# Writing out the loops of a decoder layer's attentions, expert tiles and combining

## The chip, the cores and the metric

One core of a Trainium2 chip runs the whole kernel. Its engines are TensorE (PE; its weight loads are listed as PEld), VectorE (DVE), ScalarE (ACT), GpSimd (POOL) and SyncE (SP). Each has its own instruction stream, and they meet only at semaphores. The metric is the device time in microseconds. The kernel before takes 1984.65 us, the median of three runs between 1984.55 and 1985.22.

## The reference

One decoder layer with post-norm, on 32 sequences of 64 tokens of width 512 (2048 tokens), in float32:

```python
x = layernorm(x + self_attention(x))        # 32 heads of 16, causal, biases
x = layernorm(x + cross_attention(x, ctx))  # 32 query heads, 8 key heads of 128, rotary
x = layernorm(x + moe(x))

def moe(x):                                 # 16 experts, 4 per token, inner width 256
    scores = sigmoid(x @ gate_w.T) + bias
    topk_w, topk_idx = top_k(scores, 4)
    topk_w = topk_w / (sum(topk_w) + 1e-20)
    out = sum over the token's experts of topk_w * (silu(x @ Wg.T) * (x @ Wu.T)) @ Wd.T
    return out + (silu(x @ Sg.T) * (x @ Su.T)) @ Sd.T
```

## The kernel before, in words

Every float32 factor of a product is split into two float16 parts, and three matmuls stand for one product (`three_pass`, L382 to L384). The kernel runs in stages, one after the other:

1. `self_attention`: 4 groups of heads, and in each 4 steps of 512 tokens (`NG` = 4, `NQ` = 4).
2. `cross_attention`: 8 key heads with 4 query heads each (`NG` = 8), again 4 steps of 512 tokens.
3. `layernorm`, then `route_and_shared`: the gate, the lists of tokens per expert and the shared expert.
4. `experts`: 80 tiles of 128 gathered rows, in `NR` = 20 rounds of `U` = 4. Weights lie in a ring of four experts' places in SBUF. A tile's place in the ring is data: TensorE loads it into a register (`place_of`, L1996) and forms each weight slice's address from it.
5. `combine_and_normalise`: 16 tiles of 128 tokens, in 4 rounds of 4. For each tile a DMA brings four rows per token. VectorE and ScalarE weigh them, GpSimd adds ScalarE's two, and VectorE normalises the tile before.

The order of work on each engine is written by hand. In a step of the attentions TensorE's front work (projections, scores) is mixed with the back work (transposes, values, output product) of the step before. Loops over head groups, over rounds of tiles and over rounds of combining are hardware loops: `eng.Fori(a, b)` emits the body once per engine, followed by an addition on a counter and a compare-and-branch to the body's head. Each engine loops by itself and no barrier lies between iterations. The inner loop over `q` is Python's and is written out.

What a wait compares with is computed by class `Timeline`: each event has a place in the body, and `value(name, step)` gives `step.i * n + n + place + 1`. Where `step.i` is a loop's counter, this is an expression of a register, and it costs register instructions (ALU_OP, FUSED_REGOPS in the trace) ahead of the waiting instruction. Where `step.i` is a number, it is a constant. The same holds for addresses such as `m.place[0:1, bass.ds(column, 1)]`.

In self-attention the last group stands after the loop (`step(NG - 1, q, True)`), since it carries the first layer norm. In cross-attention the first group stands ahead of the loop for the same reason. So TensorE's loop passes are three in self-attention (two taken branches and an exit, L929), seven in cross-attention (six taken, L1389) and twenty in the experts (nineteen taken, L1998). GpSimd's steps in self-attention and SyncE's loading of experts are written out already.

Steps that the prediction follows: TensorE's tile in `experts`, where `gate_and_up` is followed by `turn_rows` (the next tile's tokens, L1459), by `down` of the tile before and by `turn_z` (L1992), which waits for VectorE's z (L1952). In combining they are ScalarE's `part` (Copy, L2089) and `root` (Sqrt, L2080), GpSimd's addition (L2073), and VectorE's L2129, L2139 and L2122.

Of the kernel before, what the change touches and what calls it, by code (L numbers as in the profile page):

```python
# [27 lines left out]
NQ = NT // TQ  # L28
# [80 lines left out]
def build(nc, x, xT, cT, maskf, wqT, wkT, wvT, b3, woT, bo, xwq, xwk, xwv, xwo,  # L109
# [3 lines left out]
    with top:  # L113
# [284 lines left out]
        def self_attention(prefetch_ctx, next_front, next_out, next_keys, next_values, ln):  # L398
# [3 lines left out]
            with ExitStack() as ctx:  # L402
# [67 lines left out]
                @block.sync  # L470
                def _(sp):
                    def front_weights(g):
                        for n, w in enumerate((wkT, wqT, wvT)):
                            sp.dma_start(raw_f[:, :, n * P:(n + 1) * P],
                                         w.rearrange("(k p) n -> p k n", p=P)[:, :, bass.ds(g * P, P)]).then_inc(s_rf, 16)
                    for h in range(2):
                        sp.dma_start(stage[0][:, 2 * h:2 * h + 2, :],
                                     xT.rearrange("(k p) t -> p k t", p=P)[:, 2 * h:2 * h + 2, 0:QT]).then_inc(s_st[h], 16)
                    front_weights(0)
                    sp.dma_start(ident[:, :], eye).then_inc(s_cn, 16)  # L480
                    sp.dma_start(caus[:, :], causal).then_inc(s_cn, 16)
                    sp.dma_start(par[:, :], parity).then_inc(s_cn, 16)
                    sp.dma_start(rawb[:, :, :], b3).then_inc(s_rb, 16)
                    sp.dma_start(raw_o, woT[0:P, :]).then_inc(s_ro, 16)
                    sp.wait_ge(s_pre_v, 1)
                    with sp.Fori(0, NG - 1) as i:
                        front_weights(i + 1)
                        sp.wait_ge(DV.sem, DV.value("wol", Step(i, 0)))
                        met(sp)
                        sp.dma_start(raw_o, woT[bass.ds((i + 1) * P, P), :]).then_inc(s_ro, 16)  # L490
                        sp.wait_ge(DV.sem, DV.value("wvl", Step(i, 3)))
                        met(sp)
                    next_front(sp, s_rf)
# [102 lines left out]
                def _(act):  # L596
# [74 lines left out]

                    with act.Fori(0, NG - 1) as i:
                        for q in range(NQ):
                            step(i, q)
                    for q in range(NQ):
                        step(NG - 1, q, True)
                    done = Step(None, 0)
# [10 lines left out]
                def _(dve):  # L688
# [103 lines left out]

                    with dve.Fori(0, NG - 1) as i:
                        for q in range(NQ):
                            step(i, q)
                    for q in range(NQ):
                        step(NG - 1, q, True)
                    done = Step(None, 0)
# [17 lines left out]
                def _(pe):  # L816
# [111 lines left out]

                    with pe.Fori(0, NG - 1) as i:  # L929
                        for q in range(NQ):  # L930
                            step(i, q)
                    for q in range(NQ):
                        step(NG - 1, q, True)
                    done = Step(None, 0)
# [16 lines left out]
        def cross_attention(cs, sn, s_cn, s_ro, PE, ln):  # L951
            NG = HKV
            FW = GQ * HD2 + 2 * HD2
            with ExitStack() as ctx:
# [54 lines left out]
                @block.sync  # L1009
                def _(sp):  # L1010
                    def front_weights(g):
                        c = 0
                        for w, n in ((xwq, GQ * HD2), (xwk, HD2), (xwv, HD2)):
                            sp.dma_start(raw_f[:, :, c:c + n],
                                         w.rearrange("(k p) n -> p k n", p=P)[:, :, bass.ds(g * n, n)]).then_inc(s_rf, 16)
                            c += n

                    def out_weights(g):
                        sp.dma_start(raw_o[:, :, :], xwo[bass.ds(g * GQ * HD2, GQ * HD2), :]
                                     .rearrange("(h p) n -> p h n", p=P)).then_inc(s_ro, 16)  # L1020
# [12 lines left out]
                    sp.sem_inc(s_cw, 32)  # L1033
                    sp.dma_start(rawc[:, :], ew[0:P, 0:CH]).then_inc(s_cr, 16)
                    with sp.Fori(0, NG) as i:
                        nxt = (i + 1) % NG
                        front_weights(nxt)
                        for q in range(NQ):
                            if q == 1:
                                sp.wait_ge(DV.sem, DV.value("wol", Step(i, 1)))  # L1040
                                met(sp)
                                out_weights(nxt)
                            sp.wait_ge(DV.sem, DV.value("cl", Step(i, q)))
                            met(sp)
# [13 lines left out]
                def _(pool):  # L1058
# [18 lines left out]

                    for q in range(NQ):
                        step(0, q, True)
                    with pool.Fori(1, NG) as i:  # L1080
                        for q in range(NQ):
                            step(i, q)

                @block.scalar
                def _(act):
# [75 lines left out]

                    for q in range(NQ):
                        step(0, q, True)
                    with act.Fori(1, NG) as i:
                        for q in range(NQ):
                            step(i, q)
                    back_p(Step(None, 0))
# [3 lines left out]
                def _(dve):  # L1171
# [114 lines left out]

                    for q in range(NQ):
                        step(0, q, True)
                    with dve.Fori(1, NG) as i:
                        for q in range(NQ):  # L1290
                            step(i, q)
                    st = Step(None, 0)
# [5 lines left out]
                def _(pe):  # L1298
# [87 lines left out]

                    for q in range(NQ):
                        step(0, q, True)
                    with pe.Fori(1, NG) as i:  # L1389
                        for q in range(NQ):  # L1390
                            step(i, q)
                    st = Step(None, 0)
# [442 lines left out]
        def experts(m):  # L1835
# [5 lines left out]
            with ExitStack() as ctx:  # L1841
# [40 lines left out]
                def _(pool):  # L1882
# [7 lines left out]
                    def store(st, i, first):  # L1890
# [10 lines left out]
                                                None).then_inc(s_yo[slot], 16)  # L1901
                    with pool.Fori(0, NR) as i:
                        for q in range(U):
# [14 lines left out]
                def _(act):  # L1918
                    AC.start(act)
                    with act.Fori(0, NR) as i:  # L1920
                        for q in range(U):
# [16 lines left out]
                def _(dve):  # L1938
# [9 lines left out]
                    with dve.Fori(0, NR) as i:  # L1948
                        for q in range(U):
# [14 lines left out]
                def _(pe):  # L1964
# [32 lines left out]

                    with pe.Fori(0, NR) as i:  # L1998
                        for q in range(U):
# [14 lines left out]
                            before = w  # L2014
                    down(Step(None, 0), weights(place_of(NTILES)))

        def combine_and_normalise(m):

            with ExitStack() as ctx:
# [17 lines left out]
                def _(sp):  # L2037
# [29 lines left out]
                def _(pool):  # L2067
                    PO.start(pool)
                    with pool.Fori(0, NQ) as i:  # L2069
                        for q in range(TQ):  # L2070
# [5 lines left out]
                def _(act):  # L2076
# [4 lines left out]
                    AC.start(act)  # L2081
                    with act.Fori(0, NQ) as i:
                        for q in range(TQ):
# [11 lines left out]
                def _(dve):  # L2095
# [18 lines left out]
                    def normalise(st, tile):  # L2114
# [8 lines left out]
                                                  ALU.subtract, ALU.mult), "norm", st)  # L2123
                    with dve.Fori(0, NQ) as i:
                        for q in range(TQ):
# [146 lines left out]
```

## Time and profile before

| | |
|---|---|
| median of three runs | 1984.65 us |
| the profiled execution | 1981.03 us, its span 1979.2 us |
| TensorE matmul busy | 1751.4 us (88%), 15496 instructions |
| VectorE busy | 1353.7 us (68%) |
| ScalarE busy | 940.9 us (48%) |
| GpSimd busy | 936.9 us (47%) |
| granted TensorE clock, mean | 0.95 |
| DMA | 200.13 MB, mean 101 GB/s |

The shares are means over stages that have different limits, so the rows below are taken stage by stage. Times are from the span's start. A granted clock of 1.00 is TensorE's upper level, 0.50 its lower. Matmuls are pipelined: the next starts before the end that is drawn for the one before it. Register, branch and semaphore instructions are not counted as busy; the view by line lists them, with a q behind the engine's name.

### The profile page before, as it was taken

The page shows a single profiled execution, that of the slowest core. Times are in us where ns is not written, and L with a number is a line of the kernel's source. Part 1 is how long each engine was busy: PE and PEld are TensorE (multiplying, and loading weights), DVE is VectorE, ACT ScalarE, POOL GpSimd, SP SyncE. Part 2 cuts the span into 40 slices and gives each one's busy share as a digit, 9 for nine tenths or more (in the row PEclk, how much of TensorE's full clock was granted, in tenths as well). Part 3 has the DMA queues.
Part 4 walks back from the last instruction along what each step waited for, and adds up shares of the span by engine and source line. Part 5 has one row for each costly group of instructions (what it writes and reads, how often), then busy time and mean ns, then how long its engine had stood idle before and what let it go on. Part 6 is the DMA issues. An engine that isn't in the chain of part 4 may idle for free. (4 is left out here: it accounts for less than half of the span.)

```text
span 1979.2 us, 45274 instructions
## 1 busy us (share of the span) xinstructions
PE 1751.4 (88%) x15496; PEld 1004.4 (51%) x15497; DVE 1353.7 (68%) x2069; ACT 940.9 (48%) x1565; POOL 936.9 (47%) x905
## 2 busy tenths in 40 slices
PE   6999999899999999999999999964678999999910
PEld 4666776555555555555555555533234554555500
DVE  5777888778788788887878888776753333333357
ACT  4556557654555654645545555434222333333334
POOL 6732024564554554645645546514344454445432
PEclk9999999999999999999999999986889999999965
DMA  9520011112221121221312203121313454643369
GB/s 265 124 44 24 3 56 50 54 65 76 75 90 61 65 97 54 97 78 41 118 44 85 86 33 118 65 72 54 106 64 129 141 205 168 220 151 111 111 235 311
DMA packets 82510, 200.13 MB, mean 101 GB/s; under 512 B 8704, under 2 KB 28544, under 8 KB 80320
## 3 DMA queue, kind: packets, MB, share of 16 engines
q1 hardware_dynamic: 63456, 136.89, 20.4%
q0 software_dynamic: 18912, 61.09, 9.9%
q8 instruction: 120, 1.97, 0.4%
q14 instruction: 22, 0.18, 0.0%
HBM read 141.86 MB, written 56.10 MB: 100 GB/s over the span
## 5 line engine op out<-in xcount | busy, mean ns | idle before, releaser
L382 PE MATMUL bank<-xhl,front_h 128*128 128x512 f16 x704 | 270.2, 384 | 20.5 <-DVEq L68 13.1
L383 PE MATMUL bank<-xhl,front_h 128*128 128x512 f16 x704 | 270.2, 384 | 0.0
L384 PE MATMUL bank<-xhl,front_l 128*128 128x512 f16 x704 | 269.9, 383 | 0.0
L1067 POOL TENSOR_TENSOR xa_xs<-xa_xs,sn 128x512 f32<-128x512 f32 x160 | 233.5, 1459 | 59.2 <-ACT xa_xs L1110 59.1
L1072 POOL TENSOR_TENSOR xa_rr<-xa_x,xa_xs 128x512 f32<-128x512 f32 x160 | 232.1, 1450 | 34.0 <-POOL xa_xs L1067 24.0
L1075 POOL TENSOR_TENSOR xa_sc<-xa_sc,xa_rs 128x1024 f32<-128x1024 f32 x32 | 62.2, 1945 | 374.2 <-DVE xa_rs L1281 374.2
L382 PE MATMUL bank<-out_h,xa_oh 128*128 128x512 f16 x512 | 194.2, 379 | 7.4 <-DVE xa_ol L1186 7.3
L383 PE MATMUL bank<-out_l,xa_oh 128*128 128x512 f16 x512 | 194.0, 379 | 0.0
L384 PE MATMUL bank<-out_h,xa_ol 128*128 128x512 f16 x512 | 194.0, 379 | 0.0
L1201 DVE TENSOR_TENSOR xa_x<-bank,cs 128x512 f32<-128x512 f32 x160 | 109.9, 688 | 84.7 <-ACT xa_xs L1110 82.5
L1109 ACT ACTIVATE xa_xs<-bank 64x512 f32<-64x512 f32 x160 | 95.0, 593 | 130.8 <-PE bank L384 127.2
L1952 DVE SCALAR_TENSOR_TENSOR mo_z<-bank,mo_sg 128x256 f32<-128x256 f32 x80 | 34.0, 425 | 179.7 <-ACT mo_sg L1924 174.3
L1900 POOL DMA_INDIRECT scratch_y<-mo_yo,mo_rows_to x81 | 80.0, 987 | 133.7 <-DVE mo_zl L1959 68.4
L1157 ACT ACTIVATE xa_sc<-xa_sc 128x512 f32<-128x512 f32 x64 | 40.2, 629 | 214.9 <-DVE xa_sc L1221 214.9
L382 PE MATMUL bank<-moe_ring,moe_xth 128*128 x320 | 123.1, 385 | 14.4 <-ACT mo_yo L1933 7.1
L1206 DVE TENSOR_TENSOR xa_rql<-xa_rr,xa_rqh 128x512 f16<-128x512 f32 x128 | 114.2, 892 | 14.4 <-ACT xa_rqh L1116 12.6
L383 PE MATMUL bank<-moe_ring,moe_xth 128*128 x320 | 122.3, 382 | 0.0
L384 PE MATMUL bank<-moe_ring,moe_xtl 128*128 x320 | 122.3, 382 | 0.0
L1924 ACT ACTIVATE mo_sg<-bank 128x256 f32<-128x256 f32 x80 | 30.7, 384 | 192.6 <-PE bank L384 190.1
L1193 DVE SCALAR_TENSOR_TENSOR acc<-bank,acc 128x512 f32<-128x512 f32 x128 | 86.1, 673 | 51.8 <-PE bank L384 51.8
L382 PEld LDWEIGHTS bank<-xhl,front_h 128*128 128x128 f16 x704 | 69.6, 99 | 100.6 <-DVEq L68 12.9
L384 PEld LDWEIGHTS bank<-xhl,front_l 128*128 128x128 f16 x704 | 69.6, 99 | 85.1 <-issue 3.8
(308 smaller groups left out, 4929.2 us busy)
## 6 DMA issues: line engine op xcount, KB each, us to landing
xa_rawc<-in_ew SPq DMA_DIRECT2D x33, 768.0 KB, 5.0
moe_ring<-scratch_w SPq DMA_DIRECT2D x16, 1536.0 KB
co_rows<-scratch_y SPq DMA_DIRECT2D x20, 1024.0 KB, 7.7
scratch_w<-xa_chunk_h SPq DMA_DIRECT2D x32, 384.0 KB, 2.3
scratch_w<-xa_chunk_l SPq DMA_DIRECT2D x32, 384.0 KB, 3.1
raw_front<-in_xwq SPq DMA_DIRECT2D x9, 1024.0 KB, 7.2
raw_out<-in_xwo SPq DMA_DIRECT2D x9, 1024.0 KB, 5.2
out<-raw_front SPq DMA_DIRECT2D x17, 256.0 KB, 6.7
```

The source lines that it names most:

```text
L382: pe.matmul(out_ap, ah, bh, start=start and m == 0, stop=False)
L383: pe.matmul(out_ap, ah, bl, start=False, stop=False)
L384: mm = pe.matmul(out_ap, al, bh, start=False, stop=stop and m == n - 1)
L1067: PO.mark(pool.tensor_tensor(xr, xr, sn[:, :].rearrange("p (a s) -> p a s", a=1) .to_broadcast([P, QT // S, S]), ALU.mult), f"sm{r}", st)
L1072: PO.mark(pool.tensor_tensor(rr[r % 2][:, :], x0[r % 3][:, :], xs[r % 3][:, :], ALU.add), f"ra{r}", st)
L1075: PO.mark(pool.tensor_tensor(s4, s4, rs[:, :, :].rearrange("p h (t a) -> p (h t) a", a=1) .to_broadcast([P, 16, S]), ALU.mult), "nm", st)
L1109: act.activation(xs[r % 3][0:64, :], src[64:128, :], ACT.Copy)
L1157: AC.mark(act.activation(s2, s2, ACT.Exp, scale=float(HD2) ** -0.5), f"ex{h}", st)
L1193: DV.mark(dve.scalar_tensor_tensor(row, home[f"w{t}"][:, :], 1 / (WS * OS), row, ALU.mult, ALU.add), f"w{t}", st)
L1201: DV.mark(dve.tensor_tensor(xr, home_of(r, st)[:, :].rearrange("p (a s) -> p a s", s=S), cs[:, :].rearrange("p (a s) -> p a s", a=1) .to_b ...
L1206: DV.mark(dve.tensor_tensor(rotated(rkl, rql, r), rr[r % 2][:, :].rearrange("p (a s) -> p a s", s=S), rotated(rkh, rqh, r), ALU.subtract), ...
L1900: pool.indirect_dma_start(ys[:, :], bass.IndirectOffsetOnAxis(rows_to[slot][:, 0:1], 0), yo[slot][:, :], None).then_inc(s_yo[slot], 16)
```

## The change

The hardware loops of the two attentions, of the experts' tiles and of combining become Python loops, on every engine that has one there. The loops of the two layer norm helpers stay. In both attentions the group that stood apart joins the others, with the same steps in the same order. In the experts TensorE no longer loads the tile's place a second time at the start of each round, nor once more after the last tile: it keeps the register.

```diff
@@ self_attention, SyncE
-                    with sp.Fori(0, NG - 1) as i:
+                    for i in range(NG - 1):
@@ self_attention, ScalarE, VectorE and TensorE alike
-                    with pe.Fori(0, NG - 1) as i:
+                    for i in range(NG):
                         for q in range(NQ):
-                            step(i, q)
-                    for q in range(NQ):
-                        step(NG - 1, q, True)
+                            step(i, q, i == NG - 1)
@@ cross_attention, SyncE
-                    with sp.Fori(0, NG) as i:
+                    for i in range(NG):
@@ cross_attention, GpSimd, ScalarE, VectorE and TensorE alike
-                    for q in range(NQ):
-                        step(0, q, True)
-                    with pe.Fori(1, NG) as i:
+                    for i in range(NG):
                         for q in range(NQ):
-                            step(i, q)
+                            step(i, q, i == 0)
@@ experts, GpSimd, ScalarE, VectorE and TensorE alike
-                    with pe.Fori(0, NR) as i:
+                    for i in range(NR):
@@ experts, TensorE
-                            if q == 0:
-                                before = weights(place_of(i * U))
+                            if (i, q) == (0, 0):
+                                before = weights(place_of(0))
...
-                    down(Step(None, 0), weights(place_of(NTILES)))
+                    down(Step(None, 0), before)
@@ combine_and_normalise, SyncE, GpSimd, ScalarE and VectorE alike
-                    with sp.Fori(0, NQ) as i:
+                    for i in range(NQ):
```

## Rows read from the trace of the kernel before

**Rows 1.** windows by stage: length, busy time per engine, PEclk, DMA share, GB/s
```profile
23.00:325.00 302.00, 284.83 (x4820) 200.01 (x4817) 238.98 (x414) 178.96 (x305) 116.04 (x159) 0.99 0.25 64
325.00:1313.00 988.00, 963.04 (x7632) 537.27 (x7630) 787.62 (x1010) 539.69 (x843) 522.79 (x352) 0.99 0.22 73
...
1500.00:1890.00 390.00, 376.65 (x2240) 199.35 (x2238) 140.38 (x280) 128.06 (x280) 192.31 (x323) 0.99 0.46 157
1900.00:1979.00 79.00, 0.00 (x0) 0.00 (x0) 59.95 (x116) 36.04 (x57) 22.94 (x16) 0.50 0.92 322
```

**Rows 2.** view by line, TensorE's loop branches: ns min/median/max, first and last start
```profile
L929 PEldq COMPARE_BRANCH  x3: 76/4243/4771, 91.0 to 243.7; - x3
...
L1389 PEldq COMPARE_BRANCH  x7: 83/3602/3903, 575.3 to 1300.6; - x7
...
L1998 PEldq COMPARE_BRANCH  x20: 76/208/228, 1517.6 to 1886.8; - x20
```

**Rows 3.** timeline of TensorE, where head groups begin: start us, us, engine line op
```profile
95.99 0.48 PE L382 MATMUL bank<-xhl,front_h 128*128 128x512 f16 x1 [2.92 <-DVE acc L728]
...
173.08 0.39 PE L382 MATMUL bank<-xhl,front_h 128*128 128x512 f16 x1 [2.38 <-DVE acc L728]
...
245.37 0.38 PE L384 MATMUL bank<-out_h,sa_ol 128*128 128x512 f16 x1
245.58 0.38 PE L382 MATMUL bank<-xhl,front_h 128*128 128x512 f16 x1
```

**Rows 4.** windows, behind the first edge (as rows 1)
```profile
96.00:100.00 4.00, 4.00 (x11) 1.47 (x12) 1.09 (x1) 0.00 (x0) 3.71 (x5) 0.57 0.30 89
```

**Rows 5.** waits of TensorE, 457 to 1300 us: us in total, times, longest
```profile
PE bank L382 <- DVE xa_sc L1221: 2.5, 5, 0.7
```

**Rows 6.** timeline of TensorE at two tile starts; last, the group's mean ns
```profile
1537.42 0.38 PE L1992 MATMUL bank<-ident,mo_z 128*128 128x128 f32 x2
1538.20 0.39 PE L382 MATMUL bank<-moe_ring,moe_xth 128*128 x1 [0.40 <-issue]
...
1542.54 0.38 PE L1992 MATMUL bank<-ident,mo_z 128*128 128x128 f32 x2
1542.85 0.39 PE L382 MATMUL bank<-moe_ring,moe_xth 128*128 x1
...
L1992 PE MATMUL bank<-ident,mo_z 128*128 128x128 f32 x160 | 30.8, 274 | 0.0
```

**Rows 7.** view by line, from z to the next tile (as rows 2)
```profile
L1952 DVE SCALAR_TENSOR_TENSOR mo_z<-bank,mo_sg x1: 424/424/424, 1541.4 to 1541.4; 128x256 f32<-128x256 f32 x1
...
L1996 PEldq TENSOR_LOAD <-moe_place x1: 301/301/301, 1542.0 to 1542.0; - x1
```

**Rows 8.** view by line, ScalarE in combining (columns as in rows 2)
```profile
L2089 ACT ACT_TABLE_LOAD  x4: 1283/1283/1283, 1905.7 to 1953.7; - x4
...
L2080 ACT ACT_TABLE_LOAD  x4: 1283/1283/1283, 1908.4 to 1956.4; - x4
```

**Rows 9.** timeline of VectorE in combining
```profile
1941.74 0.69 DVE L2139 TENSOR_TENSOR acc<-acc,raw_out 128x512 f32 x1 [1.06 <-POOL raw_out L2073]
...
1943.01 0.74 DVE L2129 SCALAR_TENSOR_TENSOR acc<-co_rows,moe_w,acc 128x512 f32 x1
...
1946.81 0.75 DVE L2129 SCALAR_TENSOR_TENSOR acc<-co_rows,moe_w,acc 128x512 f32 x1
```

**Rows 10.** DMA queues, 325 to 1313 us: packets, MB, share of 16 engines
```profile
q8 instruction: 70, 1.15, 0.5%
```

**Rows 11.** timeline of TensorE in the experts, at late weights
```profile
1682.55 0.62 PE L1459 MATMUL bank<-identh,moe_rows 128*128 128x128 f16 x8 [1.74 <-ACT moe_xth L1929]
```

**Rows 12.** timeline of TensorE, first 50 us; last, a window (as rows 1)
```profile
29.67 0.22 PE L383 MATMUL bank<-front_l,xhl 128*128 128x128 f16 x1 [2.21 <-issue]
...
48.22 0.20 PE L382 MATMUL bank<-sa_vbh,sa_pth 128*64 128x34 f16 x1 [1.61 <-issue]
...
47.00:52.00 5.00, 3.78 (x69) 3.74 (x70) 2.49 (x6) 0.59 (x1) 2.13 (x2) 0.66 1.02 355
```

More of the change, by code:

```diff
@@ L670, in step @@
                             AC.mark(act.activation(wo_h, raw_o, ACT.Copy, scale=WS), "woh", st)
-                    with act.Fori(0, NG - 1) as i:
+                    for i in range(NG):
                         for q in range(NQ):
-                            step(i, q)
-                    for q in range(NQ):
-                        step(NG - 1, q, True)
+                            step(i, q, i == NG - 1)
                     done = Step(None, 0)
@@ L791, in step @@
                             DV.mark(dve.scalar_tensor_tensor(wo_l, raw_o, WS, wo_h, ALU.mult, ALU.subtract), "wol", st)
-                    with dve.Fori(0, NG - 1) as i:
+                    for i in range(NG):
                         for q in range(NQ):
-                            step(i, q)
-                    for q in range(NQ):
-                        step(NG - 1, q, True)
+                            step(i, q, i == NG - 1)
                     done = Step(None, 0)
@@ L927, in step @@
                         back_out(st)
-                    with pe.Fori(0, NG - 1) as i:
+                    for i in range(NG):
                         for q in range(NQ):
-                            step(i, q)
-                    for q in range(NQ):
-                        step(NG - 1, q, True)
+                            step(i, q, i == NG - 1)
                     done = Step(None, 0)
@@ L1034, in _ @@
                     sp.dma_start(rawc[:, :], ew[0:P, 0:CH]).then_inc(s_cr, 16)
-                    with sp.Fori(0, NG) as i:
+                    for i in range(NG):
                         nxt = (i + 1) % NG
@@ L1076, in step @@
                                                    .to_broadcast([P, 16, S]), ALU.mult), "nm", st)
-                    for q in range(NQ):
-                        step(0, q, True)
-                    with pool.Fori(1, NG) as i:
+                    for i in range(NG):
                         for q in range(NQ):
-                            step(i, q)
+                            step(i, q, i == 0)
                 @block.scalar
@@ L1160, in step @@
                         AC.mark(act.activation(chunk_h[:, :], rawc[:, :], ACT.Copy, scale=WS), "ch", st)
-                    for q in range(NQ):
-                        step(0, q, True)
-                    with act.Fori(1, NG) as i:
+                    for i in range(NG):
                         for q in range(NQ):
-                            step(i, q)
+                            step(i, q, i == 0)
                     back_p(Step(None, 0))
@@ L1285, in step @@
                         DV.mark(dve.scalar_tensor_tensor(chunk_l[:, :], rawc[:, :], WS, chunk_h[:, :], ALU.mult, ALU.subtract), "cl", st)
-                    for q in range(NQ):
-                        step(0, q, True)
-                    with dve.Fori(1, NG) as i:
+                    for i in range(NG):
                         for q in range(NQ):
-                            step(i, q)
+                            step(i, q, i == 0)
                     st = Step(None, 0)
@@ L1385, in step @@
                             back_out(st, (2, 3))
-                    for q in range(NQ):
-                        step(0, q, True)
-                    with pe.Fori(1, NG) as i:
+                    for i in range(NG):
                         for q in range(NQ):
-                            step(i, q)
+                            step(i, q, i == 0)
                     st = Step(None, 0)
@@ L1901, in store @@
                                                 None).then_inc(s_yo[slot], 16)
-                    with pool.Fori(0, NR) as i:
+                    for i in range(NR):
                         for q in range(U):
@@ L1919, in _ @@
                     AC.start(act)
-                    with act.Fori(0, NR) as i:
+                    for i in range(NR):
                         for q in range(U):
@@ L1947, in out_rows @@
                         DV.mark(dve.tensor_copy(o[:, :], Y[(st.q + 1) % 2][:, :]), "y", st)
-                    with dve.Fori(0, NR) as i:
+                    for i in range(NR):
                         for q in range(U):
@@ L1996, in place_of @@
                         return pe.value_load(m.place[0:1, bass.ds(column, 1)], min_val=0, max_val=(RING - 1) * 2 * EW)
-                    with pe.Fori(0, NR) as i:
+                    for i in range(NR):
                         for q in range(U):
@@ L2068, in _ @@
                     PO.start(pool)
-                    with pool.Fori(0, NQ) as i:
+                    for i in range(NQ):
                         for q in range(TQ):
@@ L2081, in _ @@
                     AC.start(act)
-                    with act.Fori(0, NQ) as i:
+                    for i in range(NQ):
                         for q in range(TQ):
@@ L2123, in normalise @@
                                                   ALU.subtract, ALU.mult), "norm", st)
-                    with dve.Fori(0, NQ) as i:
+                    for i in range(NQ):
                         for q in range(TQ):
```

## The prediction

> **What bounds the kernel now.** Read the busy time by stage first, then TensorE's gaps inside each stage, since there it is over 94% busy in three of the four long stages [rows 1]: self-attention (23 to 325 us of the trace), cross-attention (325 to 1313) and the experts' tiles (1500 to 1890). Layer norm and routing (1313 to 1500) stay as they are. Combining (1900 to 1979) has no matmul; VectorE runs 60 of its 79 us. A loop's edge can move the end only where it holds up TensorE, or VectorE in combining. So the second view is the branch at each loop's end on TensorE's sequencer [rows 2], and the third the row in which the next step's first matmul starts [rows 3, 5, 6].
>
> The branch tells two things. Taken, it lasts 4.2 to 4.8 us in self-attention (the smallest of the three, 0.08, is the exit) and 3.6 us in the median in cross-attention, but 0.21 us in the experts' loop, whose body is short. Other engines' branches are not read as costs: what they delay would show on TensorE or, in combining, on VectorE.
>
> **Self-attention: two taken branches on TensorE.** After the first the next matmul comes 2.92 us late, after the second 2.38 [rows 3]. A 512-column matmul is drawn 0.38 us long but the next starts 0.22 later, as the two rows at 245.37 and 245.58 show, so each idle figure hides 0.16 more: 3.08 and 2.54, together 5.6. The rows name VectorE's addition (L728) as what ended the wait. I read that as the last semaphore in a list and not as the cause, for the third passage, at 245.58, has the same waits and the same splitting of weights behind it, its branch falls through, and it has no gap at all. The first gap is followed by 3.4 us in which the granted clock is one half (0.57 over the 4 us window) [rows 4], the lower of 1.2 and 2.4 GHz, after the array had stood still: half of 3.4 us, 1.7 more. Sum 7.3 us. Inside a step constants for the waits give nothing that I count, since the array has no gap there to close; a stall of a few tenths that VectorE ends would shrink by tenths at most.
>
> **Cross-attention: six taken branches.** TensorE's queue covers most of each 3.6 us: five gaps of together 2.5 us are left [rows 5], with the hidden 0.16 each 3.3; the sixth is below the view's threshold, at most 0.3. I take 3.6 us. VectorE, ScalarE and GpSimd shed register work behind TensorE, whose array is busy 963 of 988 us [rows 1]; that counts nothing, and if it ended TensorE's few other waits sooner it could give back some of these 25 us, which the low end holds.
>
> **Experts: nineteen taken branches and eighty tile starts.** At a loop's edge the first matmul of a tile starts 0.78 us after the pair of transposes before it (1537.42 to 1538.20), elsewhere 0.31 (1542.54 to 1542.85) [rows 6]: 0.47 us lost per edge, 19 edges, 8.9 us. The remaining 0.31 also has slack in it. The pair is drawn 0.38 long for two transposes of 0.27 each, so the second starts 0.11 after the first, and the next matmul could start at 0.22: 0.09 lost on each tile. The reason is on the sequencer. TensorE's sequencer sits at the wait for z until VectorE has written it (1541.4 plus 0.42, just over 1541.8), and only then computes the column of the ring's place, loads it (0.30 us) and goes on [rows 7]; the first matmul comes 1.0 us after z, while the array has 0.9 us of queued work. The computing of the column (some 0.10 with its distance to the next) goes when the column is a constant; the load itself, its bounds check and the address arithmetic for each weight slice stay. That just closes the gap: 80 times 0.09 is 7.2 us. Bounds of this term: 0, if the waits or the load become no earlier, and 7.2, as no more gap is there. I take 7.2, since the removed piece is as long as the gap. The reload of the place at each q = 0 goes too; it lies among queued matmuls and is worth nothing.
>
> Against this stands one stretch in which weights arrive late: at 1682.55 TensorE has waited 1.74 us behind ScalarE's copy, which itself waits for the ring's DMA by the code (L1926) [rows 11]. These loads run back to back at their own pace. Through their 30 us TensorE cannot keep what it gains there, six tiles of 0.09 and one edge of 0.47: minus 1.
>
> **Combining: three edges and the activation tables.** ScalarE loads a table twice per iteration, once before the first Copy (L2089) and once before the root (L2080), 1.28 us each, eight in all [rows 8]. Within an iteration Copy runs without a load after a root, so the root's table holds Copy. Only the loop's head, reached with two different tables, asks for the first load. Written out, one load before the first root is left of eight. On VectorE the edge shows as 1.06 us of idle before the addition at 1941.74, released by GpSimd [rows 9], which got its operands late from ScalarE. An iteration lasts 16.0 us (the four loads at L2089 stand from 1905.7 to 1953.7, 48.0 over three); a step without an edge 1946.81 minus 1943.01, 3.80 [rows 9]. Four of these are 15.2: 0.8 us for each of the three edges, 2.4. The first load (1905.74) lies ahead of the first Copy after the rows have landed, and goes too: 1.3 us on the first tile. Sum 3.7. What is late next is VectorE itself, whose seven operations fill the 3.80. The DMA is close behind: 1.31 MB per tile (1024 and 256 KB) in 3.80 us is 345 GB/s; the stage moves 322 GB/s at a share of 0.92 [rows 1], full 350, 3.75 us per tile. It allows the gain by a hair, and it is the next bound.
>
> **What straight code adds.** One queue carries instructions, 70 packets of together 1.15 MB in cross-attention [rows 10]; that stage ran 15,262 matmuls and loads [rows 1], 218 per packet. I read it as TensorE's code being fetched as it goes, in loops as well, while the experts' loop, short, stayed on the engine and will now be fetched. Twice in self-attention TensorE is idle in the middle of straight code for "issue", 2.21 us before 29.67 and 1.61 before 48.22, the second with a mean clock of 0.66 over 47 to 52 us [rows 12], which I read as late fetches. Written out, the packets' ends fall elsewhere in the steps of the second to fourth head groups. One more such stall with a half clock behind it is 1.8 and 1.7 us; two in the sixteen steps are seen, both early, so for the other twelve I allow half of one, minus 2 (bounds 0 and minus 7). The experts' 4,478 matmuls and loads [rows 1] are 21 packets, one in 18 us, far longer than the longest stall of a branch, 4.77: nothing there. The Trainium skill (Runtime: NRT & Kernel Launch, Instruction fetch mechanics) has a taken branch outside a two-block window force a fetch, which the branches of rows 2 agree with, but it also has sequential fetching mostly hidden; the rows at 29.67 and 48.22 disagree, if a fetch is their cause, and by the page the sum would be 2 us larger.
>
> Another of its rules speaks against the change: a compare-and-branch takes about 108 ns (Advanced Engine Details and Errata, Control Flow Timing). By that the experts' 19 edges would give 2.1 us and not 8.9, and the sum would be 20.9. The trace has 0.21 for the branch alone and 0.47 for the edge with what follows it in line, so the rows decide.
>
> **The sum.** 7.3 + 3.6 + 8.9 + 7.2 - 1 + 3.7 - 2 = 27.7 us. The profiled execution took 1981.03 us (span 1979.2); from it 1953.3. The median of the runs is 1984.65, 3.6 above it, with runs 0.7 apart. I carry the difference over: 1957.0 us.
>
> **Rivals.**
>
> A. VectorE's releases in the attentions are real: the branch hides behind them and without it the next matmul still waits for L728 or L1221, as rows 3 and 5 name them. Then 7.3 and 3.6 go, 16.8 is left, 1967.9 us. Against it stands the passage at 245.58.
>
> B. The tile start keeps its 0.09 (the load is paced by something else than the column's arithmetic): 20.5 left, 1964.2 us. For it: the two lengths compared differ by only 0.01.
>
> C. The loops' bodies hid fetching. With every engine streaming its code while the experts' DMA is 0.46 busy [rows 1], each of the 21 packets in the experts costs a stall as at 48.22 with the half clock behind it, 3.5 us: 74 lost against 27.7 won, 2031 us. It decides from 1.3 us per packet. Against it: cross-attention's 70 packets, with its DMA 0.22 busy, left the array idle for 25 us in all.
>
> D. The loops were cheap and the saved time returns in later waits of the same stages (late weights in the experts, DMA in combining): under 4 us left, about 1983.
>
> E. More than the sum: VectorE's chains in self-attention shorten as well, 35 us, about 1949.
>
> **How the numbers follow.** The forecast 0.55, A 0.12, B 0.16, C 0.05, D 0.04, E 0.08. 1957.0 is the likeliest. B and A reach to 1968; if both held, 9.6 us would be left, 1975, and I go most of the way there; E reaches to 1949. Range 1949 to 1972, which leaves out C, D and little else. A measurement of this kernel tells about 0.2%, 4 us, from no change. Faster 0.91, within it 0.04, slower 0.05.
>
> **What would show it.** No COMPARE_BRANCH of several microseconds on TensorE in the attentions; matmul following matmul at 0.22 us where the second and third head groups begin, and no half clock near 96 us. Tile period in the experts 4.56 us throughout, against 4.65 and 5.12. One table load in combining and an even 3.8 us step. The forecast is wrong if TensorE shows "issue" gaps of 1 to 4 us in the experts (C), if the gaps at the head groups stay with VectorE named (A), or if tile starts keep 0.31 us (B).

## The result and the profile after

The kernel after takes 1941.09 us in the median of six runs (1939.38 to 1943.79), the kernel before beside it 1984.54 (1980.39 to 1985.22): ratio 0.9786, interval [0.9773, 0.9798], 43.5 us less. The forecast was 1957.0 and its range 1949 to 1972, so the sign was right and the gain 16 us too small. The profiled execution of the kernel after took 1940.97 us, its span 1939.2, 40.0 less than the span before.

The table lays both profiled executions side by side. Each stretch runs between two matmuls that both kernels have. The last two columns give the same stretch in all traces of this study in which the stretch was left with its loops, and in which it was written out.

| stretch | before | after | gain | forecast | with loops | written out |
|---|---|---|---|---|---|---|
| start to self-attention's last step | 300.18 | 291.56 | 8.6 | 5.3 | 297.8 to 303.9 | 290.1 to 292.9 |
| cross-attention, second to last step | 879.63 | 871.96 | 7.7 | 3.6 | 879.1 to 879.8 | 872.0 |
| between the two | 94.29 | 94.29 | 0 | 0 | | |
| its last step, layer norm, to routing's logits | 97.75 | 98.38 | -0.6 | 0 | | |
| logits to the ranking's first matmul | 23.91 | 19.15 | 4.8 | 0 | see experiments | |
| from there to the experts' first matmul | 101.54 | 99.77 | 1.8 | 0 | 99.6 to 104.5, same code | |
| experts' matmuls | 392.85 | 378.54 | 14.3 | 15.1 | 390.8 to 393.2 | 376.8 to 378.7 |
| last matmul to the end | 89.07 | 85.52 | 3.6 | 3.7 | 88.8 to 90.5 | 84.6 to 85.6 |

The sum is 40.05 against 27.7. Windows by stage of the kernel after (columns as in [rows 1]) show self-attention in 293 us with 283.6 busy, and the clock whole in the experts:

```profile
23.00:316.00 293.00, 283.57 (x4828) 201.22 (x4827) 238.57 (x414) 178.99 (x306) 117.47 (x161) 0.99 0.27 67
316.00:1292.00 976.00, 956.92 (x7629) 535.50 (x7625) 811.72 (x1008) 537.63 (x841) 522.15 (x352) 1.00 0.22 73
...
1480.00:1854.00 374.00, 367.17 (x2235) 197.85 (x2233) 140.93 (x280) 128.18 (x280) 191.18 (x320) 1.00 0.48 164
1854.00:1939.00 85.00, 0.02 (x1) 0.00 (x0) 61.34 (x117) 26.01 (x50) 24.39 (x17) 0.53 0.87 305
```

The timeline of TensorE at the second head group, answering to [rows 3], has the next step's matmul 0.22 behind the last of the old one, and the window behind it, answering to [rows 4], has the whole clock:

```profile
93.34 0.38 PE L384 MATMUL bank<-out_h,sa_ol 128*128 128x512 f16 x1
93.56 0.38 PE L382 MATMUL bank<-xhl,front_h 128*128 128x512 f16 x1
...
93.50:97.50 4.00, 4.00 (x25) 2.32 (x23) 3.96 (x6) 2.33 (x5) 3.71 (x5) 1.00 0.01 4
```

A tile of the experts, answering to [rows 6], starts 0.22 after the pair of transposes and not 0.31. In the stretch of late weights, answering to [rows 11], TensorE now waits 1.27 and 1.75 us. The view says "issue" there, but each of the two matmuls starts 0.10 us behind the end of ScalarE's copy (`moe_xth`, ending at 1648.26 and 1655.65), and no packet of instructions is under way at these times. So this is still the wait for weights and not the stall that rival C names. First the tile's start, then the two waits:

```profile
1505.24 0.38 PE L1978 MATMUL bank<-ident,mo_z 128*128 128x128 f32 x2
1505.46 0.38 PE L382 MATMUL bank<-moe_ring,moe_xth 128*128 x1
...
1648.36 0.61 PE L1445 MATMUL bank<-identh,moe_rows 128*128 128x128 f16 x8 [1.27 <-issue]
...
1655.76 0.61 PE L1445 MATMUL bank<-identh,moe_rows 128*128 128x128 f16 x8 [1.75 <-issue]
```

In combining, ScalarE's groups of instructions (last the idle time before them) hold one table load, where [rows 8] had eight:

```profile
L2075 ACT ACTIVATE raw_out<-co_rows,moe_w 128x512 f32<-128x512 f32 x32 | 21.1, 707 | 17.5 <-DMA co_rows<-scratch_y 17.5
L2066 ACT ACTIVATE co_rs<-co_mv,eps 128x1 f32<-128x1 f32 x17 | 5.0, 295 | 36.2 <-DVE co_mv L2098 36.2
L2066 ACT ACT_TABLE_LOAD x1 | 1.3, 1283 | 0.0
```

What the forecast had not looked at is routing, which the change doesn't touch. In the kernel before, TensorE stood still in the middle of its 192 matmuls of 16 columns. The timeline, then the group of these matmuls in 1368 to 1384 us (count, busy us and mean ns, idle time before them by releaser), then windows (as [rows 1]):

```profile
1376.50 0.17 PE L384 MATMUL bank<-ro_gh,xhl 128*128 128x16 f16 x1
1380.28 0.19 PE L382 MATMUL bank<-ro_gh,xhl 128*128 128x16 f16 x1 [3.60 <-issue]
...
L382 PE MATMUL bank<-ro_gh,xhl 128*128 128x16 f16 x64 | 5.3, 174 | 6.5 <-issue 3.6 <-DVE ro_gl L1668 2.9
...
1374.00:1378.00 4.00, 2.68 (x101) 2.58 (x97) 0.00 (x0) 0.51 (x1) 3.35 (x1) 0.50 0.95 300
1378.00:1386.00 8.00, 5.72 (x28) 2.34 (x29) 4.57 (x30) 1.67 (x2) 0.00 (x0) 0.50 0.33 113
```

The same views of the kernel after have 0.35 us in place of 3.60, and the clock comes back sooner:

```profile
1360.12 0.17 PE L384 MATMUL bank<-ro_gh,xhl 128*128 128x16 f16 x1 [0.35 <-issue]
...
L384 PE MATMUL bank<-ro_gh,xhl 128*128 128x16 f16 x64 | 5.3, 174 | 0.4 <-issue 0.4
...
1358.00:1362.00 4.00, 3.65 (x132) 3.51 (x129) 0.00 (x0) 0.84 (x1) 3.69 (x1) 0.50 0.98 311
1362.00:1370.00 8.00, 8.00 (x33) 3.35 (x32) 7.37 (x56) 2.26 (x3) 0.00 (x0) 0.85 0.37 130
```

### The profile page after: what moved, and what is told of

Same layout as the page of the kernel before. It is cut to its first block and busy times, and to the rows that moved or that the text cites. A ratio compares the mean times of both kernels' runs of the same rounds, so it can differ in the third digit from the quotient of the medians.

```text
span 1939.2 us, 39745 instructions
## 1 busy us (share of the span) xinstructions
PE 1737.5 (90%) x15496; PEld 1003.0 (52%) x15496; DVE 1378.6 (71%) x2069; ACT 929.0 (48%) x1557; POOL 936.8 (48%) x905
## 5 line engine op out<-in xcount | busy, mean ns | idle before, releaser
L382 PE MATMUL bank<-xhl,front_h 128*128 128x512 f16 x704 | 269.3, 382 | 18.0 <-DVEq L68 14.3
L1196 DVE TENSOR_TENSOR xa_rql<-xa_rr,xa_rqh 128x512 f16<-128x512 f32 x128 | 144.5, 1129 | 12.7 <-ACT xa_rqh L1108 12.1
```

The lines of the kernel that those rows point to most:

```text
L382: pe.matmul(out_ap, ah, bh, start=start and m == 0, stop=False)
L1196: DV.mark(dve.tensor_tensor(rotated(rkl, rql, r), rr[r % 2][:, :].rearrange("p (a s) -> p a s", s=S), rotated(rkh, rqh, r), ALU.subtract), ...
```

## Experiments: one stage at a time

Each of the first four kernels is the kernel before with the loops of one stage written out, as the diff of the change does it there. Theory 1 is that the stages keep what the traces show; theory 2, that TensorE's code is fetched in packets, and where a packet ends decides the routing's stall.

> Only self-attention is written out (all four engines and SyncE there); the other loops stay. Theory 1 (each stage keeps what the two traces show for it): the last self-attention step starts 8.6 us earlier, time about 8.6 us below the kernel before, ratio 0.9957, if the code behind it keeps its stalls. Theory 2 (the place of TensorE's code in its 16 KB packets decides the stall of 3.75 us in the routing's 16-column matmuls): the written-out code moves everything behind it, so that stall may be gone here too though routing is untouched; then 12 us, ratio 0.994. The prediction on record: 5.3 us, 0.9973.

> Only cross-attention is written out. Theory 1: 7.9 us less (3.8 from the six branches, 3.4 from steps 1 of each kv head, 0.5 us each, in which TensorE waits shorter for VectorE's low half), ratio 0.9960. The prediction on record: 3.6 us, 0.9982. Theory 2 adds or not the 3.3 to 5 us of the routing's stall, by where the code comes to lie.

> Only the experts' tiles are written out. TensorE's code ahead of them doesn't move, so the routing's stall of 3.75 us stays under both theories. Theory 1: 14.3 us less, ratio 0.9928. The prediction on record: 15.1 us. If half the gain were due to the engines arriving in another phase from the routing stage (theory 3), under 8 us.

> Only combining is written out. Theory 1 and the prediction: 3.5 to 3.7 us less, ratio 0.9982. Rival: the saved table loads lie under the rows' transfers and only the edges count, 2.4 us, 0.9988. In no theory does anything ahead of combining move.

| written out | ratio, interval | median us | its own stretch, gain over before | logits' run, us |
|---|---|---|---|---|
| self-attention | 0.9927 [0.9907, 0.9947] | 1967.41 | 10.1 | 5.11 |
| cross-attention | 0.9937 [0.9917, 0.9958] | 1970.93 | 7.6 | 5.11 |
| experts | 0.9930 [0.9910, 0.9950] | 1968.92 | 14.1 | 8.58 |
| combining | 0.9979 [0.9964, 0.9994] | 1978.55 | 4.3 | 8.06 |

The kernel before ran 17 times beside them, 1973.1 to 1989.0 us, median 1981.62. The last column is the routing's 192 matmuls, 8.82 us in the kernel before and 5.61 in the kernel after. Where TensorE's code ahead of routing changed in length, the stall is gone; where it didn't, it stands. That is theory 2's mark, in a stage that the edit didn't touch. The gains of the stretches are differences of two single executions, and the traces with the loops differ among themselves by 6 us in self-attention's stretch, by 0.7 in cross-attention's and by 2.4 in the experts' (first table). The four gains add to 2.27% where the change has 2.14; the stall counts in two of them, and the intervals are wider than the rest.

## Experiments: the place of the code

Both kernels get semaphore increments on TensorE behind cross-attention's last matmul, and nothing else:

```
                     back_out(st)
+                    for _ in range(128):   # 159 in the kernel after
+                        met(pe)
```

> The kernel before, with 128 semaphore increments on TensorE's sequencer behind cross-attention's last matmul, where TensorE waits for layer norm anyway: half a 16 KB packet of 256 instructions. In the kernel before, the stall of 3.75 us stands at the 353rd instruction of the routing's 384 fast ones (192 matmuls of 16 columns and their weight loads, one instruction per 13.3 ns). Theory 2 (a packet ends there, and the next was asked for only 256 instructions, 3.4 us, earlier, and waits behind the weights' transfers): the packet's end moves to the 225th, the one behind it lies outside the fast run, no stall in the run, which takes 5.1 us and not 8.8, and from the last layer norm transposes to the ranking's first matmul 25.3 us pass and not 28.6 to 30.2. Rival (the stall belongs to the transfers or to a wait the trace doesn't show): it stays, near the same time after the run's start.

> The kernel after, with 159 such increments at the same place. There a gap of 0.50 us stands at the 256th instruction. Theory 2: the packets' ends move to the 97th and 353rd, as in the kernel before, and the stall of 3 to 3.8 us comes back, the run takes 8.1 to 8.8 us and not 5.6, the stretch 28.6 to 30.2 us and not 25.3, although every loop is written out. Rival (writing the loops out removed the stall in some other way): no stall, 25.3 us.

The groups of the same matmuls, first of the kernel before moved by 128 instructions, then of the kernel after moved by 159:

```profile
L382 PE MATMUL bank<-ro_gh,xhl 128*128 128x16 f16 x64 | 5.2, 174 | 3.2 <-DVE ro_gl L1670 3.2
```

```profile
L382 PE MATMUL bank<-ro_gh,xhl 128*128 128x16 f16 x64 | 5.3, 175 | 5.7 <-DVE ro_gl L1656 2.9 <-issue 2.8
```

The loops are all there in the first, and its run takes 5.11 us without a stall; the loops are all gone in the second, and the stall is back, the run 8.10 us. From the last transposes of layer norm to the ranking's first matmul pass 26.4 and 28.9 us (25.3 expected, and 28.6 to 30.2). So the stall belongs to the code's place and not to the loops. Over all 18 traces the rule holds: seven with TensorE's code at the old place have 8.1 to 8.9 us, ten with it elsewhere 5.1 to 6.6, and the one put back 8.10. In all eight that have the stall it stands before the 178th of the 192 matmuls (2.9 to 3.8 us from start to start). In the four whose TensorE code ahead of it is that of the kernel after, a shorter gap (0.5 to 1.5 us) stands before the 129th; the other six have none. The expectation was wrong on a side matter: the increments start 0.15 us apart, 19.5 and 24.4 us in all. The wait for layer norm hides only some 5 us of that, and the routing's matmuls began 14.7 and 19.9 us later. The times, 1994.21 and 1966.61 us, are so not the stall's price.

The next one moves the whole stream of the kernel after by 105 instructions from its head, to free self-attention's start, where the stalls of [rows 12] remain; beside it ran the kernel after, unchanged.

```
                     PE.start(pe)
+                    for _ in range(105):
+                        met(pe)
                     pe.wait_ge(s_q0l, 2)
```

> The kernel after with 105 semaphore increments ahead of TensorE's first wait, where it has over 15 us to wait for the first weights: all ends of packets lie 105 instructions earlier. In the kernel after the stalls at 31.42 us (2.46) and 49.03 (1.24) stand at the 449th and 962nd instruction of TensorE's stream, 513 apart, both one instruction off the same place in a packet of 256. Theory 2 (a packet's end inside a run of short matmuls costs the fetch's time less the run's): the ends move to places 344, 600, 856, 1112, of which only the first lies in a run, 4.2 us behind the one before it; both stalls and the routing's 0.50 go and none of over 1 us comes: 3 to 6 us less than the kernel after, about 1936. Rival (the stalls are the transfers', or others appear in their place): 1939 to 1943 or more.

> The kernel after, unchanged, beside the one with the shifted code on the same chip: 1938 to 1944 us by its six runs.

The timelines of TensorE in the kernel after (two rows) and in the moved one:

```profile
31.42 0.22 PE L384 MATMUL bank<-front_h,xhl 128*128 128x128 f16 x1 [2.24 <-issue]
...
49.03 0.20 PE L384 MATMUL bank<-sa_vbh,sa_ptl 128*64 128x34 f16 x1 [1.08 <-issue]
```

```profile
31.03 0.20 PE L383 MATMUL bank<-sa_vbl,sa_pth 128*64 128x34 f16 x1 [0.69 <-issue]
```

The two stalls are gone, one of 0.84 (0.69 of it drawn as idle above) and one of 0.60 us have come, and the routing's run is 5.12. The time didn't fall: 1945.38 us (1941.53 to 1946.34) against 1942.79 (1937.95 to 1944.36), ratios to the kernel before 0.9809 [0.9789, 0.9829] and 0.9788 [0.9766, 0.9810], which overlap. The trace says why: the increments take 0.15 us each there, more than the wait that should cover them, and the first matmul starts at 17.24 us and not at 13.10. The mechanism came out as told, the gain didn't, and a version that wins by it was not found.

## Experiments: which engine's loop

In cross-attention, written out on TensorE alone, on all but TensorE, and on GpSimd alone:

```
-                    with pe.Fori(1, NG) as i:      # pool.Fori for GpSimd alone
+                    for i in range(NG):
```

> Cross-attention written out on TensorE only; the other engines keep their loops. Measured by the trace, from the first matmul of the second step to that of the last (879.6 us in the kernel before, 872.0 written out on all). Theory 1 (two separate parts: TensorE's own branches 3.8 us, the other engines' shorter step 1 3.4 us): 875.8 us here. Rival (all of it is TensorE's, its own constants included): 872.0. Rival (the branch hides behind VectorE, as row A of the prediction had it): 879.

> Cross-attention written out on GpSimd, ScalarE, VectorE and SyncE, TensorE keeps its loop. Same stretch. Theory 1: 876.2 us, and each kv head's step 1 is 30.38 long instead of 30.86. Rival (all of it is TensorE's): 879.6 and 30.86.

> Cross-attention written out on GpSimd only. From the second step's first matmul to the last step's: 879.3 to 879.8 us in eight kernels with the loops, 878.3 with TensorE alone written out, 873.4 with all but TensorE. Theory 1a (GpSimd's rotation, which had 0.23 us of register work between two of its operations and hands VectorE its sums late, sets step 1 of each kv head): 875.5 to 876.5 here, step 1 at 30.43 and not 30.86. Theory 1b (VectorE's own loop does): 879 to 880 and 30.86.

Measured: 878.34, 873.43 and 873.40 us, against 879.6 and 872.0. TensorE's branches are worth 1.3 us while the other loops stay. Their cost moves rather than goes: the steps at an edge, 30.09 to 30.65 us long before, are 29.79, but the ones after them, mostly 29.79 before, are 30.28. GpSimd's loop alone is 6.2 of 7.7 us. Its timeline in the kernel before, where the addition follows the product 0.23 us after its end, and in the kernel after, where it follows in 0.08:

```profile
673.64 1.27 POOL L1067 TENSOR_TENSOR xa_xs<-xa_xs,sn 128x512 f32<-128x512 f32 x1 [1.52 <-ACT xa_xs L1110]
675.15 1.27 POOL L1072 TENSOR_TENSOR xa_rr<-xa_x,xa_xs 128x512 f32<-128x512 f32 x1 [0.23 <-POOL xa_xs L1067]
```

```profile
663.18 1.27 POOL L1061 TENSOR_TENSOR xa_xs<-xa_xs,sn 128x512 f32<-128x512 f32 x1 [1.53 <-ACT xa_xs L1102]
664.53 1.26 POOL L1066 TENSOR_TENSOR xa_rr<-xa_x,xa_xs 128x512 f32<-128x512 f32 x1
```

Between the two stand three register instructions that compute the counts for its waits. Five such pairs make a step, 0.75 us. TensorE feels it in step 1 of each key head (steps are counted from 0 here and below), where it waits for VectorE's low half at the output products. The waits of TensorE, 457 to 1250 us, first before, then with only GpSimd written out:

```profile
PE bank L382 <- DVE xa_ol L1186: 5.9, 8, 1.3
```

```profile
PE bank L382 <- DVE xa_ol L1184: 4.4, 8, 1.1
```

Step 1 goes from 30.86 to 30.43 us, as theory 1a said, and the steps at an edge are 29.9 to 30.0, nearly without it, which the theory had not expected: the row of [rows 5] (VectorE L1221, 2.5 us) and one at L1178 (1.2 us) are gone from this view, though TensorE still takes its six branches. The trace of before has VectorE's name on these waits; the slow link is one engine further up.

Self-attention written out on TensorE only, and combining on ScalarE only:

> Self-attention written out on TensorE only. From the start of the second step to that of the last: 263.5 to 266.4 us in seven kernels with the loops, 254.4 to 255.2 in three written out on all. Theory 1, the prediction's (the two taken branches on TensorE with the half clock behind them, 7.3 us): 257 to 259, with steps 3 and 7 at 17.9 to 18.2. Rival (the branches of VectorE, ScalarE and GpSimd hold TensorE when its own is gone, as in cross-attention): steps 3 to 8 keep half or more of the 8 to 11 us, 260 to 263. Row A of the prediction (it all stays with VectorE): 263 or more.

> Combining written out on ScalarE only. From the last matmul to the end: 89.1 to 90.5 us in eight kernels with the loops, 84.8 and 85.5 written out on all. Theory 1 (the table loads and ScalarE's own branch make the edge late): 84.8 to 86 us. Rival (only the first table load counts, 1.3 us, the edges are VectorE's, GpSimd's and SyncE's branches): 87.6 to 88.5.

Self-attention: 259.93 us, at the lower end of the rival's range, but its step 1 was odd (23.94 us; in the other traces 18.5 to 22.5). Steps 3 to 8, which hold both edges, tell more: 116.6 us in the mean of ten traces with the loops (112.6 to 118.7), 109.5 with TensorE alone written out, steps 3 and 7 at 18.28 and 17.99, and 107.8 in the mean of seven written out on all (107.6 to 108.1). TensorE's two branches with their half clock are 7.1 us (7.3 were put on them), the other engines' loops 1.7. The 109.5 is one trace, and the ten with the loops spread over 6 us, so the parts are good to a few us; steps 3 and 7 alone, 19.7 to 21.4 us in those ten, bear out that both edges go. Rival A's reading falls here. Combining: 86.50 us, between theory and rival: of some 4.3 us ScalarE gives 3, the other loops the rest. ScalarE's groups already have the one table load that the kernel after has:

```profile
L2089 ACT ACTIVATE raw_out<-co_rows,moe_w 128x512 f32<-128x512 f32 x32 | 21.1, 707 | 17.1 <-DMA co_rows<-scratch_y 17.1
L2080 ACT ACTIVATE co_rs<-co_mv,eps 128x1 f32<-128x1 f32 x17 | 5.0, 295 | 37.5 <-DVE co_mv L2112 37.5
L2080 ACT ACT_TABLE_LOAD x1 | 1.3, 1283 | 0.0
```

## Experiments: the experts' edge and tile start

> The experts' tiles written out on TensorE only. Measured by the trace, from the first matmul on the ring's weights to the last matmul: 391.1 to 393.2 us in five kernels with the loop, 376.8 to 378.7 in three with all engines written out. Theory 1 (edge and tile start are TensorE's own, as the prediction had it): 377 to 379 us. Rival (as cross-attention showed, a good part of an edge is the other engines' branches): the 19 edges keep about half of their 0.47 us, 381 to 384 us.

> The kernel after, but with the column of the ring's place computed from a register on TensorE for every tile again (register times 4 plus a constant, the register is zero), then loaded as before. Same stretch, 376.8 to 378.6 us in the kernel after. Theory 1 (the arithmetic of the column after z is what cost 0.09 us per tile, 80 tiles): 384 to 386 us, and tile periods of 4.64. Rival (the load's other parts or the registers in the waits): 377 to 379.

> The kernel after, but TensorE's loop over the experts' tiles has two iterations, each with half of the tiles written out, so that the column of the ring's place and the counts in its waits come from a register again, with one edge in place of nineteen. First matmul on the ring's weights to the last matmul, 376.8 to 378.7 us written out. Theory 1 (the register instruction of 0.11 us between z and the place's load costs each tile its 0.09 us): 384 to 387 us, most tile periods 4.64. Rival (the 0.09 comes from the distance to the branch or from something else): 377 to 380, periods 4.55.

The second and third change TensorE's loop in the kernel after:

```
-                    for i in range(NR):
+                    with pe.Fori(0, 1) as zero:             # second kernel
+                      for i in range(NR):
...
-                            w = weights(place_of(i * U + q + 1))
+                            w = weights(place_of(zero * U + (i * U + q + 1)))
```

```
-                    for i in range(NR):
+                    with pe.Fori(0, 2) as half:             # third kernel
+                      for ii in range(NR // 2):
+                        i = half * (NR // 2) + ii
```

TensorE alone: 378.53 us, all of the 14.3; here no other engine's loop counts. The second: 376.79, which looked like the rival but told nothing, for its trace has no register instruction ahead of the place's load; the constant zero had been folded away. The third has that instruction again: most periods are 4.64 to 4.68 us in place of 4.55, and every fourth tile, which reloads the old place, 4.77. So a register instruction of 0.11 us between z and the load costs each tile 0.09, as forecast. (The counts of its waits come from a register again as well, but in the trace none of those instructions stands between z and the load.) The stretch took 399.39 us, beyond what the theory allowed, because of the one branch it still has. Its duration (ns min/median/max), the two stalls on TensorE and the window:

```profile
L1984 PEldq COMPARE_BRANCH  x2: 79/3178/6276, 1676.5 to 1878.5; - x2
...
1683.96 0.60 PE L382 MATMUL bank<-moe_ring,moe_xth 128*128 x1 [6.50 <-issue]
1689.18 0.61 PE L383 MATMUL bank<-moe_ring,moe_xth 128*128 x1 [4.62 <-issue]
...
1684.00:1688.00 4.00, 0.56 (x1) 0.50 0.87 345
```

Two tiles last 11.23 and 11.13 us, 13.1 more than two others. One taken branch of a long body, with the DMA at 0.87, so costs 13 us, more than the nineteen short ones together (9.5). Sum for this kernel: 377 + 80 x 0.09 + 20 x 0.12 + 13.1 = 399.7.

## Why the prediction fell short

The error is 15.9 us: 12.3 in the sum, 3.6 in the step from the profiled execution to the median.

**"Layer norm and routing stay as they are."** This is the step that failed first, 4.8 us and by chance 1.8 more, less 0.6 that came behind cross-attention. Of the 4.8 the stall explains some 3.2: the same stretch takes 22.8 us in the mean of the seven traces with the code at its old place, and 19.5 in the ten with it elsewhere. The rest is mostly this one execution of the kernel before, the longest of the seven. Their work stayed, their code's place didn't. The prediction had the mechanism in hand, as late fetches in self-attention, and counted it only against the change, minus 2 for stalls that new code may bring. That a stall already there may leave was not asked, and the trace's largest stall of that kind, 3.60 us for "issue" at 1380.28, was not among the rows. Shown by moving the code alone, both ways.

**"VectorE, ScalarE and GpSimd shed register work behind TensorE ...; that counts nothing."** It counted 6.2 us, on GpSimd. The clause that TensorE's array is busy 963 of 988 us was true and left 25 us. Three rows of waits for VectorE held 9.6 of them, 5.9 at step 1, 2.5 in [rows 5] and 1.2 at L1178; with GpSimd's loop alone written out the first is 4.4 and the other two no longer appear. So the gaps that the prediction charged to TensorE's branches alone needed GpSimd's lateness too. Conversely TensorE's own branches, 3.6 forecast, were 1.3 alone.

**Self-attention's 7.3.** The branches measured 7.1. The minus 2 for new stalls didn't come true (from step 3 on they are even, 17.9 to 18.1 us, but for the last, 18.73 as before), and the others' loops gave 1.7. The start, up to step 2, differs by up to 4 us between executions of one code and can't be charged.

**Experts, 15.1 against 14.3.** The nineteen edges (0.5 each, 0.12 of it the place's reload, which the prediction held for nothing, 0.35 the branch) and the tile starts (0.09 each, now shown) were right. The instruction queue has 23 packets there where 21 were forecast, and no stall of rival C's size. Some tiles now begin 0.15 to 0.65 us late, some 4 us in all beyond the late weights; their cause stays open, for no run was made for it.

**Combining, 3.7 against 3.5 to 4.3.** Right, with one load of eight left.

**The offset of 3.6 us.** The profiled execution of before lay under its median, that of after at its own, 1940.97 to 1941.09. Seventeen runs of the kernel before spread over 16 us. In the traces most of it arises before self-attention's step 2 and between the ranking and the experts. It was an accident of one execution and not a property to carry over. Without it the forecast would have been 1953.3, which still misses by 12.

Of the rivals, A fell by experiment in self-attention; in cross-attention it was partly right, since the waits that name VectorE were real there and TensorE's branches alone gave 1.3 of the 3.6. B fell by experiment, C and D by the size of the gain. E had the nearest time, 1949, with the wrong engine and stage.

## What to carry to other kernels

Count what a code change does to code that it doesn't touch: look for "issue" stalls in runs of short matmuls everywhere in the trace, and give them a term of either sign. The label alone doesn't tell a late fetch, as the experts' two late weights show. An engine far from the bound counts when its chain ends in one of the bounding engine's waits, so follow the named releaser one engine further up before calling register work free. A difference between one profiled run and the median is noise until several traces show it.

## What the runs showed of the hardware

TensorE's code comes in packets of 16,384 bytes on the instruction queue. In the kernel after, the self-attention's stalls stand behind the 449th and 962nd recorded instruction, 513 apart, or twice 256 and one. In the routing's run one instruction takes 13.3 ns, so 256 last 3.4 us. The gap there, 0.5, is behind the 256th: if the packet behind it was asked for at the first (1356.19), its transfer began 1.3 us later (1357.51), took 1.3, and the first instruction ran 1.3 after that, at 1360.12, together 3.9 us. In the kernel before, asked for at the 97th (1373.1) with the DMA at 0.95, it began 4.8 us later, which gives the 3.75. The time of asking is inferred, the rest is in the traces. The Trainium skill (Runtime: NRT & Kernel Launch, Instruction fetch mechanics) has the next block of 256 instructions fetched while the current one runs, with the cost of crossing "mostly hidden". The distances agree; hidden it is only where 256 instructions last longer than the fetch, which 16-column matmuls don't.

The second surprise is the granted clock behind such a stall: in the routing of the kernel before it stayed at 0.50 up to 1386 us, 5.7 us past the stall, and in the two-iteration kernel it was 0.50 through the second stall. What that costs depends on what follows. In the two-iteration kernel long matmuls follow, which start 0.43 us apart and not 0.22, and 13.1 us were lost around 11.1 of idle. In routing no cost beyond the stall is shown: the clock is at 0.50 in the runs without a stall too, and in the mean of the traces with and without it the run of short matmuls differs by 3.1 us and the whole stretch by 3.2.
